# Cross-attention and routed feed-forward on one core: score products in pairs on the two halves of the array's rows, and a softmax denominator spread by its reciprocal

## What is computed

```python
x = x + xattn(layernorm(x), ctx, ctx, q_w, q_b, ..., o_w, o_b)
x = x + ffn(layernorm(x), router_w, gate_w, up_w, down_w)

# xattn: heads of d = 16, each query sees the 65 keys q-64..q
q = rope(query @ q_w.T + q_b) * d ** -0.5
k = rope(key @ k_w.T + k_b);  v = value @ v_w.T + v_b
scores = einsum('bhqd,bhqwd->bhqw', q, k_win)      # masked outside 0..S_k-1
e = exp(scores - max(scores));  probs = e / sum(e)
ctx = einsum('bhqw,bhqwd->bhqd', probs, v_win)
return ctx @ o_w.T + o_b
```

## Time and profile before

| | |
|---|---|
| median of three runs | 505.75 us (503.86 to 505.89) |
| the profiled execution, its own time | 506.29 us |
| its span | 504.5 us |
| PE busy | 447.6 us (89%) |
| DVE busy | 300.3 us (60%) |
| ACT busy | 271.1 us (54%) |
| score products, L420, x128 records | 54.9 us busy, 510 ns each |
| masks, L418, x64 | 23.5 us busy in the attention stage, 368 ns each |

### The profile page before, as it was taken

The page is one execution under the profiler, slowest core; times in us unless marked ns, Lnnn a source line. Parts: engine busy times, 40 slices in busy tenths (PEclk is TensorE's granted clock), DMA queues, the critical chain, the costliest instruction groups (busy, mean ns, idle before and its releaser), DMA issues.

```text
span 504.5 us, 8809 instructions
## 1 busy us (share of the span) xinstructions
PE 447.6 (89%) x2747; PEld 367.2 (73%) x2747; DVE 300.3 (60%) x727; ACT 271.1 (54%) x853; POOL 121.2 (24%) x118
## 2 busy tenths in 40 slices
PE   3998999999999998208999999999999999999970
PEld 2655675666666554207999999999999999999970
DVE  3464769797797966752754737547376473763320
ACT  2286677787768688303545545455454453554230
POOL 5301014151523304550004022040220401204013
PEclk9999999999999999556999999999999999999995
DMA  7165201020201111138665446645466453213003
GB/s 236 26 205 175 96 18 52 21 64 9 59 20 48 37 31 50 49 85 272 237 198 87 159 127 152 198 80 168 124 154 195 76 171 85 34 38 38 1 0 36
DMA packets 24317, 49.36 MB, mean 98 GB/s; under 512 B 5368, under 2 KB 15160, under 8 KB 24140
## 3 DMA queue, kind: packets, MB, share of 16 engines
q10 hardware_dynamic: 7886, 26.44, 17.0%
q1 hardware_dynamic: 10238, 15.36, 10.0%
q0 software_dynamic: 6144, 6.97, 8.5%
HBM read 38.51 MB, written 12.74 MB: 102 GB/s over the span
## 4 chain that ended last, share of the span: by engine, by line
PE 73%; DVE 7%; ACT 6%; POOL 4%; issue 3%; DMA 3%; ACTq 1%; SPq 0%; DVEq 0%; POOLq 0%
PE b_small L634 9%; PE b_o L634 9%; PE b_s L621 8%; PE b_s L622 8%; PE b_s L623 8%; PE b_s L420 5%; ACT probs L743 4%; PE b_proj L498 3%; PE b_pv L443 3%; PE b_pt L623 3%; PE b_pt L621 3%; PE b_pt L622 3%; POOL slots L1142 3%; PE b_pt L429 3%; PE b_proj L474 2%
## 5 line engine op out<-in xcount | busy, mean ns | idle before, releaser
L743 ACT ACTIVATE probs<-b_s,negmax 100x100 f32<-100x100 f32 x256 | 85.7, 361 | 23.3 <-DVE negmax L994 20.4
L1182 POOL DMA_INDIRECT out<-y_sb,idnow x32 | 47.0, 1468 | 187.1 <-ACT y_sb L784 179.7
L772 ACT CAST h_hi<-h_sb 128x448 fp32r<-128x448 f32 x64 | 36.3, 567 | 86.5 <-DVE h_sb L1085 86.5
L621 PE MATMUL b_s<-x_hi,w_hi 128*128 128x448 f32 x192 | 72.5, 378 | 0.7 <-DVE x_lo L1075 0.7
L622 PE MATMUL b_s<-x_lo,w_hi 128*128 128x448 f32 x192 | 71.6, 373 | 0.0
L623 PE MATMUL b_s<-x_hi,w_lo 128*128 128x448 f32 x192 | 71.4, 372 | 0.0
L972 DVE TENSOR_TENSOR w_lo<-w_raw,w_hi 128x1024 fp32r<-128x1024 f32 x48 | 58.4, 1224 | 13.8 <-ACT w_hi L707 13.8
L1089 DVE TENSOR_TENSOR h_lo<-h_sb,h_hi 128x448 fp32r<-128x448 f32 x64 | 40.1, 626 | 40.5 <-ACT h_hi L772 40.5
L743 ACT ACTIVATION_READ_ACCUMULATOR probs<-b_s,negmax 100x1 f32 x256 | 56.7, 222 | 0.0
L420 PE MATMUL b_s<-kblk,qrot 128*100 128x400 f32 x128 | 54.9, 510 | 0.0
L994 DVE TENSOR_REDUCE negmax<-b_s 100x4 f32<-100x400 f32 x64 | 36.2, 565 | 26.8 <-PE b_s L420 26.1
(11 more groups left out here) (131 smaller groups left out, 929.7 us busy)
## 6 DMA issues: line engine op xcount, KB each, us to landing
w_raw<-in_ffw ACTq DMA_DIRECT2D x48, 512.0 KB, 4.0
xin<-slots SPq DMA_DIRECT2D x9, 449.8 KB, 4.5
slots<-in_padrows SPq DMA_DIRECT2D x8, 449.8 KB, 4.6
kblk<-krot SPq DMA_DIRECT2D x128, 12.5 KB
out<-x_all SPq DMA_DIRECT2D x8, 200.0 KB
ctx_all<-in_ctxT SPq DMA_DIRECT2D x1, 1200.0 KB, 6.5
x_all<-in_x SPq DMA_DIRECT2D x1, 1200.0 KB
attw<-in_wT ACTq DMA_DIRECT2D x2, 256.0 KB, 3.8
```

Source lines behind the costliest of these rows:

```text
L621: pe.matmul(o, wh[:, c, cols], x_hi[:, c, :], start=(c == 0), stop=False)
L743: m = nc.scalar.activation(probs[:, N % 3, h, :], b_s[N % 3][0:S, h * S:(h + 1) * S], ACT.Exp, bias=negmax[:, N % 4, h:h + 1], accum_out=p ...
L1182: G.indirect_dma_start(out, bass.IndirectOffsetOnAxis(idnow[:, n:n + 1], 0), y_sb[:, n, :], None, bounds_check=TOK + TILE - 1, oob_is_err= ...
```

## The change

There are two edits. The score products of two quads that lie in one chunk (heads 0 to 3 and heads 4 to 7 of it) are issued together, at even n: both masks first, each into its own bank, then both products, each over the 64 rows of its own heads. The key tile drops from eight head columns to four, since both halves of the rows now use the same columns. And `den` takes the reciprocal of the row sums repeated 16 times in one instruction, without the small reciprocal and the copy.

```diff
-        rden = sb("rden", [S, 2, H])
...
-        kblk = att_sb("kblk", [P, 2, DC, HC, PT])
+        kblk = att_sb("kblk", [P, 2, DC, QH, PT])
...
-                        sp.dma_start(kblk[r, i % 2, c, h, :],
+                        sp.dma_start(kblk[r, i % 2, c, h % QH, :],
...
             def scores(i, n):
-                N = NQ * i + n
                 b, s = quad(n)
                 c = s * QH // HC
-                h = s * QH % HC
                 if n == 0:
                     pe.wait_ge(s_qrot, i + 1)
                 if n in (0, HC // QH):
                     pe.wait_ge(s_kblk[c], 16 * HC * (i + 1))
-                if N >= 3:
-                    pe.wait_ge(s_p, N - 2)
-                o = b_s[N % 3][0:S, 0:QH * S]
-                pe.matmul(o, ident_bf[0:S, 0:S], mask_bf[0:S].rearrange("p h s -> p (h s)"),
-                          start=True, stop=False)
-                pe.matmul(o, qrot[:, i % 2, 2 * c + b, :],
-                          kblk[:, i % 2, c, h:h + QH, b * S:(b + 1) * S],
-                          start=False, stop=True).then_inc(s_s, 1)
+                banks = []
+                for m in range(2):
+                    N = NQ * i + n + m
+                    if N >= 3:
+                        pe.wait_ge(s_p, N - 2)
+                    banks.append(b_s[N % 3][0:S, 0:QH * S])
+                    pe.matmul(banks[m], ident_bf[0:S, 0:S], mask_bf[0:S].rearrange("p h s -> p (h s)"),
+                              start=True, stop=False)
+                for m in range(2):
+                    r = slice(m * P // 2, (m + 1) * P // 2)
+                    pe.matmul(banks[m], qrot[r, i % 2, 2 * c + b, :],
+                              kblk[r, i % 2, c, :, b * S:(b + 1) * S],
+                              start=False, stop=True).then_inc(s_s, 1)
...
-                    if cur:
+                    if cur and n % 2 == 0:
                         scores(i, n)
...
             def den(r):
                 v.wait_ge(s_p, 4 * r + 4)
-                link(V.reciprocal(rden[:, r % 2, :], psums[:, r % 2, :]))
                 if r:
                     v.wait_ge(s_rT, r)
-                V.tensor_copy(rdenx[:, :, :], bc(rden[:, r % 2, :].unsqueeze(2), [S, H, DH])).then_inc(s_rx, 1)
+                V.reciprocal(rdenx[:, :, :], bc(psums[:, r % 2, :].unsqueeze(2), [S, H, DH])).then_inc(s_rx, 1)
```

## The result

The changed kernel takes 514.64 us (median of 4 runs, 513.53 to 515.9) against 505.82 for the kernel before beside it: a ratio of 1.0181, 95% interval 1.0137 to 1.0224. The prediction said 508.2 with a range up to 513. Taken singly, the pair of products and the reciprocal cost about what was forecast; the time that the pairs were to save did not come, because a wait that the prediction had overlooked holds the pairs back, and the half clock came, which the sum had left to a rival.

A forecast was written before the change was run, and what follows sets the result against it. It took a loop through TensorE and VectorE to bound each steady pair, lengthened from 22.41 to 22.95 us. Six periods of +0.54 (+3.2) less 0.7 gave +2.5 on 505.75: 508.3, said as 508.2, range 501.5 to 513.

The forecast's parts named there:

- The new loop: Attention stage, steady pair of sequences, through VectorE and TensorE: steps summing to 22.95 us against 22.41, +0.54 a pair.
- R(6) to S(0): From quad 6's maxima on VectorE to quad 0's score product on TensorE: 2.38 us, set by quad 6's exponentials.
- S(0) to S(2): TensorE, quad 0's score product to quad 2's: 6.51 us, less 0.89, plus mask 0.17 and switches 0.26: 6.05.
- R(5) to R(6): VectorE, quad 5's maxima to quad 6's, with `den` between: 3.99 us becomes 5.08.
- S(0) cannot start earlier than R(6) + 2.38: Quad 1's mask, ahead of quad 0's product, waits for quad 6's exponentials: 0.60 + 1.44 + 0.34 us after quad 6's maxima.
- the mask before S(0) waiting for exponentials: Sign of a right forecast: on TensorE, the mask ahead of quad 0's score product waits for ScalarE's exponentials.
- If nothing else happened, the period would be 21.8: TensorE's part of the old loop, with paired score products: 12.09 us becomes 11.47, the period 21.8 instead of 22.41.
- The overlap of the row halves: TensorE's two 64-row score products overlap fully: 0.67 us for both, plus 0.26 for entering and leaving the mode.
- The rival without overlap: Row halves do not overlap: quad 0's to quad 2's product grows 0.67, period 23.6, total 512.5 us; chance 0.12.
- the cheap reciprocal: `den`'s reciprocal costs 0.3 us: TensorE's loop sets 21.8, -0.6 a pair, 501.5 us; chance 0.25, shared with an overlong loop.
- The clock: TensorE's clock halves in the new waits: about 1.5 us in each of six pairs, 517 us; chance 0.08.
- The ends: First and last pair of sequences, where TensorE's saving counts in part: -0.7 us, between +0.8 and -2.2.

The follow-up runs named there:

- pairs_S0_first: Changed kernel with the old `den`, score products of quads 0 and 1 ahead of the previous pair's quad-4 value products: 512.23 us, 1.0125 of the kernel before.
- early_R3: Kernel before, with quad 3's maxima on VectorE moved from behind `choose` to right behind `k_rotate`: 505.14 us, ratio 0.9988.
- after_again: Changed kernel, unchanged, run again on the last chip: 515.07 us, 1.0175 of the kernel before.
- pairs_busy: Changed kernel with the old two-instruction `den`, plus filler products on TensorE where it was idle: 507.74 us, 1.0024 of the kernel before.
- after_busy: Changed kernel plus filler products on TensorE where it was idle: 513.5 us, 1.0123 of the kernel before.
- pairs_full_rows: Changed kernel with the old `den` and the large key tile, both products of a pair over all 128 rows: 513.79 us, 1.0087 of the kernel before.
- halves_single: Kernel before, with each score product on its 64 rows of the narrow key tile, one quad at a time, old `den`: 527.28 us, ratio 1.0362.
- pairs_again: Changed kernel with the old two-instruction `den`, without fillers, on the last chip: 512.75 us, 1.013 of the kernel before.

## Why the prediction was wrong

The steady pair was forecast at 22.95 and took 23.60. By the steps of "The new loop", as the timelines above have them:

| step | forecast | measured | |
|---|---|---|---|
| R(6) to S(0) | 2.38 | 2.71 | wrong wait |
| S(0) to S(2) | 6.05 | 6.16 | size |
| S(2) to R(2) | 0.88 | 0.95 | size |
| R(2) to R(3) | 5.29 | 5.45 | size |
| R(3) to R(5) | 3.27 | 3.13 | size |
| R(5) to R(6) | 5.08 | 5.20 | size |

- **The first failed step is "S(0) cannot start earlier than R(6) + 2.38", taken as what sets S(0).** The bound by E(6) was right as a bound (2.37 in pairs_S0_first), but it does not set S(0) in the changed kernel, where the mask waits for nothing: V(4) stands ahead of both masks and waits for `attend`. `attend` starts its last part 1.26 after R(6), V(4) follows at 1.77, the masks at 2.24, S(0) at 2.71. The working took from before that S(0) stood at R(6) + 2.47 "because TensorE was full". Full it was, but `attend` was as late. In the kernel before its last part starts 1.27 after R(6) at 128.64, and V(4) 1.80 after:

```profile
129.91 0.38 DVE L905 TENSOR_TENSOR att<-ev 128x200 f32<-128x200 f32 x1
...
130.44 0.53 PE L443 MATMUL b_pv<-probsT,v_sb 100*32 100x200 f32 x4
```

  early_R3 shows the wait for it as soon as TensorE comes a little earlier. So the sign "the mask before S(0) waiting for exponentials" did not come: in the profile after it is V(4) that waits, for `attend`. This step is 0.33 of the 0.65 us that the pair was off; the sizes are the rest.
- **The same omission made "If nothing else happened, the period would be 21.8" wrong.** Two loops of 22.4 ran through the old pair. The second contains R(6) to S(2), 8.98 us. The pairs should have cut it to 8.43 and cut it to 8.87: S(1) left it, and a mask, the switches and V(4)'s wait took its place. That is why the pairs of products bring next to nothing, over 64 rows or over 128, and why `den`'s growth is paid almost in full: with R(5) to R(6) 1.21 longer, the pair grew by 1.19.
- **The reciprocal was mis-sized by 5%.** 1.743 us against 1.66; `den` is +1.21 on R(5) to R(6), not +1.09. The group in the trace after:

```profile
L892 DVE RECIPROCAL rdenx<-psums 100x256 f32<-100x256 f32 x16 | 27.9, 1743 | 1.5 <-ACT probs L745 1.5
```

  It was right that the `den` after R(1) is hidden on VectorE (R(2) still waits 1.37 for scores); 0.18 of it comes out behind R(2), where `attend` waits for `rdenT`, in the rows above. The Trainium skill ("VectorE: DVE Perf Modes") has a repeat count of 8 for the reciprocal, at 0.96 GHz 8.3 ns an element, which the prediction turned into an estimate of 2.28 us; 256 elements in 1.743 us are at most 6.8 ns each, so the run does not agree with it.
- **The overlap of the row halves was right,** with its switches: 0.85 for two products as for one, 0.27 for the mode. The rival without overlap is out, and so is the cheap reciprocal. That the rival without overlap had a period of 23.6 too is chance: its cause was another. The Trainium skill ("TensorEngine Tiling (Array Packing)", Tiling Modes) says that a change of mode drains the engine; by the reading above, this case puts 0.27 us on entering and leaving.
- **The clock was a rival with 0.08, and it came,** from the waits that the prediction itself had forecast: it compared 1.15 us of idle time with the earlier trace rows, where a whole microsecond was empty, and took less to be safe. TensorE was in fact idle for 2.93 us a pair. Inside the stage the stretches were fewer and cheaper than the rival's: one that cost 1.8 us in the profile after, four that cost 0.2 to 0.4 each in after_again.
- **The ends were -0.7 and cost time.** Outside the five inner periods the changed kernel lost 2.5 us, 1.5 of it after the last R(6). These 1.5 go with the place of the half clock at the end of the stage, not with the edits: after_again, the same kernel, has 311.9 us there. No run was made to move that place alone. Of the 6.9 us by which the profiled difference (9.4) exceeds the forecast's 2.5, 4.5 lie in the six periods (1.8 of them the half clock) and 2.4 at the ends.

On the last chip the loss of 8.39 us (after_again 515.07, before 506.68) splits so by the medians: pairs of products with fillers, at full clock, 1.06 (pairs_busy less before); the long reciprocal 5.76 (after_busy less pairs_busy); the clock, less the fillers' own work, 1.57 (after_again less after_busy). By the ratios the three are 1.2, 5.0 and 2.6 us. Only the second is well above what a measurement can tell.

## What to carry to other kernels

Where three engines are each busy for over three quarters of a period, look for every loop that is as long as the period before pricing a saving: move one instruction that shortens only the loop you believe in (early_R3), and see if the period moves. Freed time on TensorE is not a gain in itself: here it became idle gaps, with these the half clock came, and filling them won back 5.0 us (pairs_busy). A product over half the rows paid only with its partner, and pairing moves the second product's wait in front of the first.

## What the runs showed of the hardware

- Two fp32 products of 64 rows and 400 columns on the two halves of the rows take 0.85 us (the profile after), as one alone does; over 128 rows one takes 0.67 and two 1.35 (pairs_full_rows). Beside a product over 128 rows, a visit to the halves costs 0.09 us more ahead and 0.18 us more behind (halves_single).
- A VectorE reciprocal of 100 x 256 elements takes 1.743 us, one of 100 x 16 takes 0.244: 6.2 ns for each further element, although each input number stands 16 times in a row.
- 1.7 us of filler products a pair made a kernel 5.0 us faster, and the granted clock, which had fallen to 0.50 four times between 60 and 190 us, stayed at 2.4 GHz there (pairs_busy and pairs_again).
